# Building a graph's adjacency: weighted cell one-hots from three TENSOR_SCALARs per unit, or from one product of tile marks and group members

## The reference, cut to what matters

```
loop = jnp.arange(n)
s = jnp.concatenate([src, loop]); d = jnp.concatenate([dst, loop])
w = jnp.concatenate([ew, jnp.ones((n,), ew.dtype)])
deg  = jax.ops.segment_sum(w, d, num_segments=n)
dinv = jnp.where(deg > 0, jax.lax.rsqrt(deg), 0.0)
norm = dinv[s] * w * dinv[d]
h    = x @ W
out  = jax.ops.segment_sum(h[s] * norm[:, None], d, num_segments=n) + b
```

## Time and profile before

| what | us |
|---|---|
| median of 3 runs (3367.15 to 3373.08) | 3372.99 |
| the profiled execution: its own time | 3363.36 |
| its span | 3361.6 |
| busy PE / DVE / ACT / POOL | 3090.0 / 1392.4 / 1419.6 / 860.8 |

### The profile page before, as it was taken

The page is one execution under the profiler, slowest core; times in us unless marked ns, Lnnn a source line. Parts: engine busy times, 40 slices in busy tenths (PEclk is TensorE's granted clock), DMA queues, the critical chain, the costliest instruction groups (busy, mean ns, idle before and its releaser), DMA issues. The chain is left out here.

```text
span 3361.6 us, 43991 instructions
## 1 busy us (share of the span) xinstructions
PE 3090.0 (92%) x13945; PEld 2037.0 (61%) x13945; DVE 1392.4 (41%) x3295; ACT 1419.6 (42%) x2520; POOL 860.8 (26%) x935
## 2 busy tenths in 40 slices
PE   5888999968898897799999799999999999999997
PEld 4775555547787786577777555555555555555554
DVE  6991111124666667699999711111111111111112
ACT  4870000223555555788888622333332223222233
POOL 2010000027777770577777300000000000000000
PEclk9998999986877877899999899999999999999999
DMA  2555667633333330666666466676676677767774
GB/s 66 208 209 232 275 283 298 263 106 77 85 81 80 80 79 24 169 191 183 184 182 182 147 276 283 279 293 284 284 293 275 283 292 300 292 275 291 292 301 164
DMA packets 163328, 709.40 MB, mean 211 GB/s; under 512 B 36427, under 2 KB 129482, under 8 KB 150055
## 3 DMA queue, kind: packets, MB, share of 16 engines
q1 hardware_dynamic: 125964, 619.72, 46.9%
q0 software_dynamic: 33920, 84.12, 10.7%
q10 hardware_dynamic: 3224, 2.75, 0.3%
HBM read 658.10 MB, written 48.07 MB: 210 GB/s over the span
## 5 line engine op out<-in xcount | busy, mean ns | idle before, releaser
L1372 PE MATMUL deep_out_psum<-deep_adjacency,deep_scaled_nodes 125*128 125x450 f32 (+1 forms) x1750 | 669.7, 537 | 0.0
L1372 PE MATMUL deep_out_psum<-deep_adjacency,deep_scaled_nodes_odd 125*128 125x450 f32 (+1 forms) x1750 | 669.7, 537 | 0.0
L1620 POOL DMA_INDIRECT source_rows<-gat_source_rows,pair_src x416 | 408.7, 982 | 576.3 <-POOLq L63 449.8
L1372 PEld LDWEIGHTS deep_out_psum<-deep_adjacency,deep_scaled_nodes_odd 125*128 125x128 f32 x1750 | 328.4, 189 | 299.8 <-issue 298.9
L1372 PEld LDWEIGHTS deep_out_psum<-deep_adjacency,deep_scaled_nodes 125*128 125x128 f32 x1750 | 328.1, 189 | 298.9 <-issue 298.0
L2188 POOL DMA_INDIRECT near_room<-gate_source_rows,pair_src x416 | 398.2, 957 | 225.3 <-issue 126.6
L1430 ACT ACTIVATE deep_squares_high<-deep_aggregate,deep_vectors 128x450 fp32r<-128x450 f32 (+1 forms) x70 | 46.8, 668 | 618.1 <-DVE deep_aggregate L1502 618.1
L2233 PE MATMUL gate_core_psum<-edge_weights,edge_features_t 128*128 128x256 f32 x832 | 260.3, 394 | 39.6 <-ACT edge_features_t L2267 39.6
L1372 PE MATMUL gcn_out_psum<-adjacency_columns,gcn_scaled_nodes 125*128 125x450 f32 (+1 forms) x700 | 268.5, 538 | 0.0
L1658 PE MATMUL score_terms_psum<-ident,source_rows 128*128 128x128 f32 x416 | 146.0, 351 | 72.4 <-issue 56.6
L1516 DVE SCALAR_TENSOR_TENSOR deep_normed<-deep_aggregate,deep_vectors,deep_squares 128x450 f32<-128x450 f32 (+1 forms) x70 | 47.9, 684 | 384.9 <-ACT deep_squares L1439 384.9
(11 more groups left out here) (409 smaller groups left out, 4724.9 us busy)
## 6 DMA issues: line engine op xcount, KB each, us to landing
deep_adjacency<-adjacency SPq DMA_DIRECT2D x69, 5625.0 KB, 16.3
adjacency_columns<-adjacency SPq DMA_DIRECT2D x19, 5625.0 KB, 16.2
adjacency<-adjacency_columns SPq DMA_DIRECT2D x7, 5625.0 KB, 17.6
edge_features<-in_edge_attr_dram SPq DMA_DIRECT2D x416, 64.0 KB
att_node_rows<-pair_dst_rows SPq DMA_DIRECT2D x104, 125.0 KB
gate_node_rows<-pair_dst_rows SPq DMA_DIRECT2D x104, 125.0 KB
source_rows<-gat_source_rows,pair_src POOLq DMA_INDIRECT x416, 2.5
near_room<-gate_source_rows,pair_src POOLq DMA_INDIRECT x416
```

The lines of the kernel that those rows point to most:

```text
L1372: m = nc.tensor.matmul(op[:, n % 2, 0:cols], h[l % 2][:, s, :], ring[0:T, n % 2, s, 0:cols], start=s == 0, stop=s == NS - 1)
L1620: pool.indirect_dma_start(xj[:, b % HOLD, q, :], None, d["h_r"], bass.IndirectOffsetOnAxis(ap=c["pair_src"][:, b * PQ + q:b * PQ + q + 1], ...
```

## The change

The table gets a fourth word, the target's member number in the group (the target's number less six times the group; 0..5 in the group, outside otherwise). POOL writes the target into the list's fourth word, DVE makes it local per gather, PE turns four words, ACT copies four. At the start of the build DVE subtracts word 3 from word 1 in place, which leaves tile*6.

The cell one-hot of 25 x 6 is then the product of a mark of the tile (25 elements) and the weighted mark of the member (6 elements). Both marks are made for CHUNK = 4 units at once, 12 groups: `members_of` (12 x 6 elements, with the second unit of the chunk before), `marks_of` (12 x 25, and the members times the weight, 12 x 6, with its third unit). The product is one TENSOR_TENSOR per unit of 3 x 25 x 6 elements that broadcasts one operand along the last dimension and the other along the middle one. The ring shrinks from 6 to 5 units, so extras are added after unit 7 of the next block; the two buffers of marks lie where the sixth unit lay and behind it. Some small buffers move into room that other tensors leave.

```diff
-        CELLS, RING, BANKS, EXTRA_AT = NS * G, 6, 6, 2
+        CELLS, RING, BANKS, EXTRA_AT = NS * G, 5, 6, 2
+        CHUNK = 4
...
+            def members_of(h):
+                lo, hi = span(h)
+                if lo < hi:
+                    n = hi - lo
+                    if h >= 2:
+                        dve.wait_ge(s_oh, (h - 1) * CHUNK)
+                    vec.tensor_tensor(members[:, h % 2, 0:n, :], c["ramp"][:, 0:G].unsqueeze(1).to_broadcast([128, n, G]),
+                                      tab[:, 3, lo:hi].unsqueeze(2).to_broadcast([128, n, G]), ALU.is_equal).then_inc(s_mb, 1)
+            def marks_of(h):
...
+                    vec.tensor_tensor(marks[:, h % 2, 0:n, :], c["ramp"][:, 0:CELLS:G].unsqueeze(1).to_broadcast([128, n, NS]),
+                                      tab[:, 1, lo:hi].unsqueeze(2).to_broadcast([128, n, NS]), ALU.is_equal)
+                    dve.wait_ge(s_mb, h + 1)
+                    vec.tensor_tensor(members[:, h % 2, 0:n, :], members[:, h % 2, 0:n, :], tab[:, 2, lo:hi].unsqueeze(2).to_broadcast([128, n, G]), ALU.mult
+                                      ).then_inc(s_mk, 1)
+            vec.tensor_tensor(tab[:, 1, :], tab[:, 1, :], tab[:, 3, :], ALU.subtract).then_inc(s_t6, 1)
+            members_of(0)
+            dve.wait_ge(s_t6, 1)
+            marks_of(0)
             for n, (b, j, u) in enumerate(units):
                 if n >= RING:
                     dve.wait_ge(s_mm, n - RING + 1)
-                g0, m, k = u[0], len(u), n % RING
+                g0, m, k, h = u[0], len(u), n % RING, n // CHUNK
+                if n % CHUNK == 1:
+                    members_of(h + 1)
+                if n % CHUNK == 2:
+                    marks_of(h + 1)
                 if n not in byact:
...
-                for q, g in enumerate(u):
-                    i = vec.tensor_scalar(cell[:, k, q, :], c["ramp"][:, 0:CELLS], tab[:, 1, g:g + 1], tab[:, 2, g:g + 1], ALU.is_equal, ALU.mult)
-                i.then_inc(s_oh, 1)
+                dve.wait_ge(s_mk, h + 1)
+                at = g0 - span(h)[0]
+                vec.tensor_tensor(cell[:, k, 0:m, :].rearrange("p q (s j) -> p q s j", j=G), marks[:, h % 2, at:at + m, :].unsqueeze(3).to_broadcast([128, m, NS, G]),
+                                  members[:, h % 2, at:at + m, :].unsqueeze(2).to_broadcast([128, m, NS, G]), ALU.mult).then_inc(s_oh, 1)
```

In `edge_lanes` one line of each kind is added, and a memset of the list's fourth word goes:

```diff
-                nc.scalar.copy(c["lane_words"][:, :, k * 128:(k + 1) * 128], p_t[:, k, 0:3, :]).then_inc(s_tab, 1)
+                nc.scalar.copy(c["lane_words"][:, :, k * 128:(k + 1) * 128], p_t[:, k, :, :]).then_inc(s_tab, 1)
...
+            g.tensor_copy(lanes[:, :, EL:128, 3], node_i[:, :, :])
...
-            g.memset(el[:, :, 3:4], 0.0)
...
+            pool.wait_ge(s_ld, 16)
+            g.tensor_copy(el[:, :, 3], ei[:, 1, :])
...
-                for w in range(3):
+                for w in range(4):
...
+                vec.tensor_scalar(lanes[:, k, 0:EL, 3], lanes[:, k, 0:EL, 3], own[:, 0, k:k + 1], None, ALU.subtract)
```

More of the change, by code:

```diff
@@ L145, in edge_lanes @@
         own = sb("own_group", [128, 2, GC])
-        ind_i = sb("block_distance_i", [128, GC, NSP], I32)
+        loose = columns[:, 0, :, :].rearrange("p s c -> p (s c)")[:, NS * D:]
+        ind_i = loose[:, 0:GC * NSP].bitcast(I32).rearrange("p (k b) -> p k b", k=GC)
         ind = sb("block_distance", [128, GC, NSP])
@@ L157, in edge_lanes @@
         lanes = spare[:, 15 * EC:15 * EC + GC * 512].rearrange("p (k e w) -> p k e w", e=128, w=4)
-        node_i = sb("self_member_i", [128, GC, G], I32)
+        node_i = loose[:, GC * NSP:GC * NSP + GC * G].bitcast(I32).rearrange("p (k j) -> p k j", k=GC)
         node = sb("self_node", [128, 2, GC, G])
@@ L379, in build_adjacency @@
         deg, safe, root, y, z = (c["h_t"][0:T, ROOM + k * NS:ROOM + (k + 1) * NS] for k in range(5))
+        MARKS = ROOM + 5 * NS
+        marks = c["h_t"][:, MARKS:MARKS + 2 * CHUNK * SUB * NS].rearrange("p (k g s) -> p k g s", k=2, s=NS)
+        members = c["h_t"][:, MARKS + 2 * CHUNK * SUB * NS:MARKS + 2 * CHUNK * SUB * (NS + G)].rearrange("p (k g j) -> p k g j", k=2, j=G)
         steps = c["dinv_b"][0:1, N - UO:N]
-        e0r = sb("extra_first_edge_f", [1, UO])
         acc = ctx.enter_context(nc.psum_tensor("adjacency_sum", [128, BANKS, 512], F32))
@@ L387, in build_adjacency @@
                  "extra_done", "columns_done", "extra_local", "degrees_copied", "extras_spread", "extras_placed", "extras_listed", "extra_step",
-                 "distances_ready", "far_onehots_ready", "degrees_summed", "degree_step", "degree_guarded", "degree_root", "dinv_ready", "dinv_turned",
+                 "distances_ready", "far_onehots_ready", "tiles_by_six", "members_marked", "marks_ready", "degrees_summed", "degree_step", "degree_guarded", "degree_root", "dinv_ready", "dinv_turned",
                  "dinv_copied")
         (s_p, s_oh, s_mm, s_ev, s_om, s_oo, s_omm, s_oc, s_od, s_blk, s_loc, s_dg, s_xs, s_xp, s_xl, s_xv,
-         s_af, s_ao, s_d, s_v, s_in, s_rt, s_n, s_t, s_c) = (c["sems"].take("build_" + n) for n in names)
+         s_af, s_ao, s_t6, s_mb, s_mk, s_d, s_v, s_in, s_rt, s_n, s_t, s_c) = (c["sems"].take("build_" + n) for n in names)
         s_st = c["adj_stored"]
@@ L442, in extras, with span @@
                 dve.sem_inc(s_blk, 1)
+            def span(h):
+                of = units[h * CHUNK:(h + 1) * CHUNK]
+                return (of[0][2][0], of[-1][2][-1] + 1) if of else (0, 0)
+            def members_of(h):
[7 more added lines that the diff above has]
+            def marks_of(h):
+                lo, hi = span(h)
+                if lo < hi:
+                    n = hi - lo
+                    vec.tensor_tensor(marks[:, h % 2, 0:n, :], c["ramp"][:, 0:CELLS:G].unsqueeze(1).to_broadcast([128, n, NS]),
[7 more added lines that the diff above has]
+            marks_of(0)
             for n, (b, j, u) in enumerate(units):
@@ L461, in _ @@
                     dve.wait_ge(s_xv, 1)
-                    vec.tensor_tensor(e0r[:, :], xps[0:1, 0:UO], steps[:, :], ALU.add).then_inc(s_xv, 1)
+                    vec.tensor_tensor(steps[:, :], xps[0:1, 0:UO], steps[:, :], ALU.add).then_inc(s_xv, 1)
                     dve.wait_ge(s_xv, 2)
-                    vec.tensor_scalar(c["extra_first"][:, :], e0r[:, :], float(E), None, ALU.min).then_inc(s_xl, 1)
+                    vec.tensor_scalar(c["extra_first"][:, :], steps[:, :], float(E), None, ALU.min).then_inc(s_xl, 1)
                 if b >= 1 and j == EXTRA_AT + RING:
@@ L2383, in graph_network @@
             c["degree_parts"] = sb("degree_parts", [NS, NSP * BW])
-            c["lane_words"] = sb("lane_words", [128, 3, 128 * GC])
+            c["lane_words"] = sb("lane_words", [128, 4, 128 * GC])
             c["extra_bounds"] = sb("extra_bounds", [1, NSP + 1], I32)
```

## The result

The changed kernel takes 3386.92 us (median of 5 runs, 3384.40 to 3387.83) against 3367.15 before (5 runs): ratio 1.0061, interval 1.0050 to 1.0071. It is slower by 0.6%, where 3362 and a gain of 11.4 us were forecast; the range, 3354 to 3371, doesn't hold it. (The forecast was counted from the first three runs before, whose median was 3372.99.) A second timing, with the later kernels on one chip, gave 1.0064 (1.0051 to 1.0078). The ratios leave out one execution of a later kernel, the one with the members in PSUM, that took 5798.65 us. The changed kernel's profiled span is 3384.1 us, 22.5 more than before, and 21.9 of them are there when the last block's store is issued.

What follows compares the result with a forecast made beforehand. DVE's pace bounds the build up to its addition at 202.95, then the store-to-store chain. Gain 14.4 (units) - 1.4 (beginning) - 1.6 (table) = 11.4 us; 3372.99 - 11.4 = 3361.6, rounded 3362; range 3354 to 3371.

Steps and rivals of the forecast that it cites:

- What bounds the kernel: Build: DVE's pace up to its addition at 202.95, then the chain from store to store for 55.1 us.
- the term for the extras in the sum: Build, from 49.89 to 202.95: 5.0 us of list and extras beside the one-hots, taken to stay.
- the chain store, load, POOL, PE, ACT, DVE, store: Build's end, from DVE's addition at 202.95: fixes the last 55.1 us, so DVE's later savings gain nothing.
- rival B: Build's blocks: chain of stores takes over earlier, four blocks wait 1 to 1.5 us each, 3367; 20 in 100.
- The product: DVE, each unit: one 450-element TENSOR_TENSOR costs 0.53 us against 0.81 for three TENSOR_SCALARs, 0.28 saved.
- The overlap: DVE in the build: the next instruction starts before the previous ends, so costs are spacings of starts, not durations.
- the rule that spoke against the change: DVE: skill's fp32 tensor_tensor formula, (N + 151)/0.96 ns without overlap; a product would cost 626 ns, the change lose.
- Rival A: DVE: overlap lost where instructions wait for their own engine's signal; unit 1.20 us, 13.3 slower, 3386; 5 in 100.
- The marks: DVE, tile and member marks: 0.70 us per four units, 0.175 per unit, with 0.38 for 300 elements.
- The beginning: Start of the build: subtraction, members, marks and weighting ahead of the first one-hot, +1.4 us; bounds 1.2 and 2.0.
- The ring: Build, five units instead of six: set at nothing; about 1 us for each of four blocks if cover is gone.
- the term for POOL: POOL's operations on the extras in the build: within the 5.0 us of list and extras taken to stay.

Runs made afterwards that it cites:

- e1: Changed kernel with the weighted member marks in a PSUM bank of their own, five banks for the sums instead of six; ratio to before 0.9988.
- e2: Changed kernel with the three small operations on an extra moved from POOL to DVE; ratio to before 1.0007.
- f2: Changed kernel with the members' marks in PSUM, timed again on a chip at the first runs' speed; 3360.41 us, ratio to before 0.9985.
- f1: The changed kernel itself, timed again on a chip at the first runs' speed; 3388.43 us, ratio to before 1.0064.
- e6: Changed kernel with the 25 tile numbers times six copied once to neighbouring elements; ratio to before 1.0044.
- e7: Kernel before with a ring of five units instead of six and nothing else; ratio to before 1.0003.
- f3: Changed kernel with members' marks in PSUM and tile numbers side by side, timed again at the first runs' speed; 3354.33 us, ratio to before 0.9972.

## Why the prediction was wrong

**What bounds the kernel** was right as far as it went: DVE's pace in the blocks, the chain of store, load, POOL, PE, ACT and DVE in the last two.

**The step that failed** is the term for the extras in the sum: "the rest of the 153.1 us since 49.89 is 5.0 us of list and extras, which stays". It did not stay. With it fell "the chain store, load, POOL, PE, ACT, DVE, store fixes these 55.1 us", and its like in rival B ("18.8 from the store to POOL ... 4.8 from POOL to the next store"). All took POOL's operations to last what they last beside the old DVE work, or beside an idle DVE. They depend on what DVE runs. In numbers:

| stretch | before | changed | forecast | measured |
|---|---|---|---|---|
| start to first row one-hot | 49.89 | 52.54 | +3.0 | +2.65 |
| to DVE's addition before the fifth store (202.95; now 219.17) | 153.1 | 166.6 | -14.4 | +13.6 |
| to the last store | 55.1 | 60.8 | 0 | +5.7 |

The middle row is 28.0 us off. DVE's waits for the sums of five extras are 17.2 of them (3.3 to 3.6 each, none before), the marks 6.9 (33 chunks at 0.91 instead of 0.70), and its other waits 2.4 (4.0 instead of 1.6); 1.5 are left over. The last row is the sixth block, where POOL needs 9.7 us for the first extra instead of 2.7. The load was as forecast (17.7 to 18.7 us from a store to POOL), and the last extra too: 4.8 from POOL to the last store. But in the second to the fifth block 12.1 to 13.8 us pass from POOL to the next store, where it was 9.3 to 11.2 before.

The old order kept POOL waiting far less, 2.5 us per extra, with three TENSOR_SCALARs per unit. In the new order every operation has two SBUF inputs, without a pause. The cost of an edit was looked for on the engine that was edited, and on what waits for it by a semaphore; the neighbour that shares a way to SBUF was not asked. Of the 21.9 us e1 takes away 24.7 and e2 20.9, and f2 against f1 28.0 us of the whole time; the wait for POOL is thus more than the whole loss, and what is left is a small gain.

The Trainium skill says so, and I had not drawn on it: "SBUF — State Buffer", section "Who interferes with whom", has a DVE instruction with two SBUF inputs contend with a GpSimd instruction that reads SBUF, and the one that comes second wait for the first to finish. The trace agrees: 7.5 us per extra against 2.2 with one input of the product in PSUM. The trace also shows what a stream of such instructions does: up to 8.8 us pass before POOL has its turn, although the products are only 0.53 us apart. By the same section TENSOR_SCALARs in a two-port mode contend too; that the old order starved POOL so much less is shown, why is not.

**The product** was right: 0.53 forecast, 0.53 measured. **The overlap** of instructions held. The product's 623 ns are near the 626 of the rule that spoke against the change, as a duration; as a spacing the rule fails. Rival A is refuted too, although its 3386 is the number that came, by coincidence: each product waits for DVE's own signal and still starts before its predecessor ends. **The marks** were sized wrong: 0.70 forecast per chunk, 0.91 measured, all of it in the 300-element operation, 0.62 instead of 0.38. It reads every sixth element of `ramp`; e6 puts them side by side and gets 464 ns. The line through the rows of before was fitted on inputs without a step. In the Trainium skill "Vector Engine (DVE) Microarchitecture Reference", section 5.2, gives 1.73 ns per element when one source hops 4 KiB at every element, and about 75 ns per instruction. A step of six words in one source is not in its table; with the figure for the hop the 300 elements would cost 0.59 us, as an estimate. The trace has 0.62.

**The beginning** was 1.62 us (50.92 to 52.54), 1.4 forecast; the whole way to the first one-hot 2.65 more than before, 3.0 forecast. That is one execution each; over all of them the new table comes 0.7 to 6.4 us later than an old one, so the agreement says little. **The ring** costs nothing in the old order, as was set (e7). In the new order DVE waits more for PE, 3.1 us up to the fifth store in f3 instead of 0.8; whether by the ring or by its own quicker pace is not separated.

With the marks quick and POOL fed, f3 comes near the sum the prediction had made: last store 9.7 us sooner than before, and 10.4 us in the medians, against 11.4 forecast. Part of that is luck. Up to DVE's addition before the fifth store (195.46) the build gains 11.6 us, not 14.4; 4.1 are lost ahead of it, not 3.0; and the stretch of 55.1 us that was called fixed is 52.9. So the arithmetic of DVE was right in kind and some 3 us too good, and the term for POOL, set at no change, was the missing 20 us and more.

**The chances**: slower had 0.07, the chain taking over (B) 0.20 with "ACT or POOL comes 2 us later". It was the right place and the wrong price: 1 to 1.5 us for each of four blocks there, 3.3 to 3.6 in each of the first five here.

## What to carry to other kernels

The cost of an operation on DVE is not only its own time. Ask which other engine reads SBUF meanwhile, above all POOL, and whether someone waits for that engine. A product that keeps one operand in PSUM left POOL free at no cost in its own time (616 against 623 ns). Where DVE runs without gaps and then waits for the very work that it keeps from SBUF, that work begins only when DVE has stopped, and the wait comes back in every block. A quicker DVE only reaches the stop sooner. And take stretches of one trace from a point inside it (here the first row one-hot): the times from the start of the span scatter by more than some of the effects.

## What the runs showed of the hardware that was not expected

- POOL's operation on 128 x 1 elements lasted up to 8.8 us beside back-to-back TENSOR_TENSORs with two SBUF inputs, and as little as 0.19 us in the same stream with one input of the product in PSUM (e1; 0.26 on average).
- In the changed kernel a starved operation of POOL ended either where a 300-element TENSOR_TENSOR with an input at a step of six elements ended (the first operation of four of six extras, to the hundredth of a us) or within 0.5 us of DVE's stop. Without the step (e6) only the stop was left.
- A TENSOR_TENSOR over 300 elements with one input at a step of six elements lasts 696 ns, and 464 without the step.
- TENSOR_TENSORs follow each other, from start to start, after 0.15 us with 72 elements, 0.46 with 375 and 0.53 with 450: about 1.0 ns per element and 0.08 us besides, also where each waits for a signal that was given long before.
- The trace doesn't tell when POOL's operation moved its data within its 3 to 9 us, only when it ended; a kernel with deliberate pauses of DVE was not tried, nor one that shows which part of the way to SBUF the two engines share.
